# Softmax stage of a four-layer graph network on one core: one product group moved ahead of an exponent product, two groups held back, and one numerator product moved to the end of the sums

## What is computed

```
w_m = (efeat @ W_msg  + b_msg ).reshape(E, 16, 16)
w_a = (efeat @ W_attn + b_attn).reshape(E, 16, 16)
h_src = feat[src][:, :, None]
e1, e2 = w_m * h_src, w_a * h_src
seg_max = segment_max(e2, dst)
ex   = exp(e2 - seg_max[dst])
ft   = segment_sum(e1 * ex / segment_sum(ex, dst)[dst], dst)
out  = ft.sum(axis=1)
```

## Time and profile before

| what | value |
|---|---|
| median of 3 runs | 10814.75 us (10812.35 to 10816.42) |
| the profiled execution | 10814.88 us, span 10812.9 us |
| PE busy | 7709.7 us, 71% |
| DVE busy | 7490.8 us, 69% |
| POOL busy | 8188.1 us, 76% |
| ACT busy | 2807.2 us, 26% |
| mean granted TensorE clock | 0.836 of full |

### The profile page before, as it was taken

How to read it: one execution, slowest core, us unless ns; L and a number is a source line. 1 busy time by engine, 2 the same in 40 slices (tenths; PEclk the granted TensorE clock), 3 DMA queues, 4 the chain that set the end, 5 groups by cost and what they waited for, 6 DMA issues and landing times.

```text
span 10812.9 us, 126451 instructions
## 1 busy us (share of the span) xinstructions
PE 7709.7 (71%) x34167; PEld 3929.5 (36%) x34167; DVE 7490.8 (69%) x13704; ACT 2807.2 (26%) x12100; POOL 8188.1 (76%) x5375
## 2 busy tenths in 40 slices
PE   0999985999946566566666656633999994788884
PEld 0455442555522222222222222211555553344442
DVE  2555551444428999999999999975778883677774
ACT  0111110000016656666666666622000000000000
POOL 5788885777758888888888888853888885788887
PEclk6999986999967777777777777765999996888886
DMA  1333331222216666666666656645222221333332
GB/s 35 97 98 98 91 81 35 62 62 62 62 24 171 172 177 178 173 175 178 174 173 178 175 172 179 176 132 181 72 75 75 75 75 29 100 90 90 90 90 49
DMA packets 501017, 1210.69 MB, mean 112 GB/s; under 512 B 244715, under 2 KB 281743, under 8 KB 480135
## 3 DMA queue, kind: packets, MB, share of 16 engines
q1 hardware_dynamic: 241732, 983.55, 28.5%
q0 software_dynamic: 223712, 118.77, 8.8%
q10 hardware_dynamic: 35440, 106.85, 3.1%
HBM read 415.09 MB, written 787.23 MB: 111 GB/s over the span
## 4 chain that ended last, share of the span: by engine, by line
POOL 37%; PE 27%; ACT 18%; issue 11%; DVE 3%; DMA 2%; SPq 1%; ACTq 0%; DVEq 0%; POOLq 0%
POOL arena L513 37%; ACT arena L726 17%; PE PS L876 10%; PE PS L1010 8%; PE PS L1011 7%; PE PS L898 1%; ACT arena L744 1%; DVE arena L1529 1%; DMA d_rel<-arena 1%; SPq L310 0%; DMA d_nn<-arena 0%; DVE arena L1561 0%; PE PS L987 0%; DVE arena L1525 0%; PE PS L1073 0%
## 5 line engine op out<-in xcount | busy, mean ns | idle before, releaser
L876 PE MATMUL PS<-arena,TB 125*128 125x500 bf16 (+1 forms) x17325 | 4103.1, 384 | 140.8 <-DVE arena L1275 138.9
L513 POOL DMA_INDIRECT arena<-d_feat,srci x1650 | 3204.6, 1942 | 730.4 <-issue 455.1
L513 POOL DMA_INDIRECT arena<-d_h,srci x1584 | 2029.1, 1281 | 697.6 <-issue 472.6
L876 PEld LDWEIGHTS PS<-arena,TB 125*128 125x128 bf16 (+1 forms) x17325 | 1570.0, 100 | 2365.1 <-issue 988.6
L726 ACT ACTIVATE arena<-PS,arena 125x32 f32<-125x32 f32 x10560 | 1934.8, 557 | 44.2 <-DMA arena<-d_feat,srci 44.2
L1010 PE MATMUL PS<-arena,ident 125*125 125x512 f32 x1650 | 1090.4, 749 | 1139.2 <-DVE arena L1529 1137.6
L1286 DVE SCALAR_TENSOR_TENSOR arena<-arena,lane,PS 128x500 f32<-128x500 f16 x825 | 598.0, 725 | 1551.0 <-PE PS L876 1180.8
L513 POOL DMA_INDIRECT arena<-d_rel,irel x858 | 1220.2, 1422 | 429.8 <-issue 261.2
L513 POOL DMA_INDIRECT arena<-d_nn,srci x858 | 1215.4, 1417 | 352.0 <-issue 261.2
L1275 DVE TENSOR_SCALAR arena<-arena,lane 125x1500 bf16<-125x1500 f16 (+1 forms) x1848 | 1191.8, 703 | 183.9 <-PE PS L876 125.5
L1561 DVE SCALAR_TENSOR_TENSOR arena<-arena 125x512 f32<-125x512 f32 x1485 | 1100.1, 741 | 0.4
(11 more groups left out here) (262 smaller groups left out, 5618.1 us busy)
## 6 DMA issues: line engine op xcount, KB each, us to landing
d_soft_den<-arena SPq DMA_DIRECT2D x330, 560.0 KB
d_soft_num<-arena SPq DMA_DIRECT2D x330, 560.0 KB
d_soft_max<-arena SPq DMA_DIRECT2D x165, 1120.0 KB
arena<-d_pick SPq DMA_DIRECT2D x99, 750.0 KB
arena<-d_lane SPq DMA_DIRECT2D x99, 750.0 KB
d_x<-arena ACTq DMA_DIRECT2D x165, 241.7 KB
arena<-d_x SPq DMA_DIRECT2D x165, 241.7 KB
d_rel<-arena SPq DMA_DIRECT2D x50, 669.4 KB
```

Source lines behind the costliest of these rows:

```text
L513: gp.indirect_dma_start(out=dst, out_offset=None, in_=table, in_offset=bass.IndirectOffsetOnAxis(ap=index, axis=0)).then_inc(S(sem), 16)
L876: ins = pe.matmul(PS[0:w, 2048 + (q % 3) * 512:2048 + (q % 3) * 512 + QW], TB[:, part, g * LANES * F:g * LANES * F + w], OH[L][i][:, g, at ...
```

## The change

On PE, the first two product groups of the next block now follow the scalable products of t = 8 and 9 and wait until DVE has done six of the 19 maxima of the current block. The third group moves from ahead of exponent difference n = 5 to ahead of n = 4. On DVE, `weigh(8)` moves from the first place of the sums to behind the sum of t = 7, so two of the interleaved places are empty at the start, and the waits of the sums are lowered by one numerator to match. No instruction is added or removed but waits.

```diff
             def soft(b, s, k, first, left):
                 ahead, k1 = (s + 1) % 3, k + (s == 2)
                 if left >= 1:
+                    for t in range(AT + 2, B1):
+                        scalable(b + 1, ahead, k1, t)
+                    pe.wait_ge(S("soft_max"), MAXES * b + AT)
                     products(b + 1, ahead, k1, 0)
                     products(b + 1, ahead, k1, 1)
-                    for t in range(AT + 2, B1):
-                        scalable(b + 1, ahead, k1, t)
 
                 for n in range(6):
                     if n == 4 and left >= 2:
                         scalable(b + 2, (s + 2) % 3, k + (s >= 1), AT)
-                    if n == 5 and left >= 1:
+                    if n == 4 and left >= 1:
                         products(b + 1, ahead, k1, 2)
...
-                weigh(B1 - 2)
+                yield
                 yield
                 weigh(0)
                 yield
...
-                        dve.wait_ge(S("soft_num"), 5 * b + 2)
+                        dve.wait_ge(S("soft_num"), 5 * b + 1)
...
-                            dve.wait_ge(S("soft_num"), 5 * b + min(t // 2 + 2, 5))
+                            dve.wait_ge(S("soft_num"), 5 * b + t // 2 + 1)
...
-                    if t % 2 and t < B1 - 3:
+                    if t % 2 and t < B1 - 1:
                         weigh(t + 1)
                         yield
```

## The result

The changed kernel takes 10494.74 us (median of 4 runs, 10489.41 to 10501.9) against 10815.58 us, a ratio of 0.9704 with a 95% interval of 0.9687 to 0.9721: 321 us or 3% faster. The forecast was 10815 us, no change. It also lies far outside the range for 8 in 10, 10776 to 10830 us. The time is close to that of the last rival, "VectorE bounds" at 10484 us, which had a chance of 0.02.

A forecast was written before the change was run, and what follows sets the result against it. The prediction took VectorE's and ACT's loops as both tight, with ACT closing the loop. From the profiled 10814.88 us, 0 x 163 + 0.7 - 0.1 gave 10815.5, rounded 10815 us; range for 8 in 10: 10776 to 10830.

The forecast's parts named there:

- VectorE bounds: Rival for the softmax stage: the gain is real, 2.03 us a block go, 331 us, giving 10484 us; chance 0.02.
- What bounds the kernel now: Softmax stage: ACT, 60% busy, closes the block loop of 23.89 us between PE's n = 3 and the maximum of t = 9.
- The 3.0 us of idle forward maxima: VectorE's forward maxima idle only 3.0 us over 2000 us, 84 blocks; read as arriving just as ACT releases them.
- two tight loops: Softmax stage: VectorE's and ACT's loops are both tight, so removing VectorE's wait leaves ACT's loop as it is.
- VectorE's wait, "Gain 0": VectorE's product instructions: the 331.5 us wait goes, but some 2 us a block of idle time appears before the forward maxima.
- The faster: Rival: the clock rises earlier or stays up at PE's differences; period 23.57, mean 23.66 us, gain 37 us, 10778; chance 0.13.
- the slower rival: Rival: PE waits for the first product pair, the exponent of n = 5 is late; period 24.16 us, 10858; chance 0.09.
- Sums before and after: VectorE: two pairs move, so products start 8.75 us after the first backward maximum instead of 7.72.
- Third group: PE, ahead of n = 4: issued 10.17 us after the first backward maximum, new wait 0.18 us, covered by ACT, cost 0.
- Numerators of t = 0: VectorE's `weigh(0)`: the exponent of n = 4 is out by then or 0.1 later, and VectorE has 2 us to give.
- First two groups held back: PE: the groups start after six maxima, where PE is idle; price 0.
- The self-restoring period: Block loop: a shorter block does more differences at 1.2 GHz before the clock's rise and gives the gain back.

The follow-up runs named there:

- the run with 18 repeats: Kernel before with 18 needless repeats of one second-group product on PE, ahead of the second group: 10664.92 us, ratio 0.9847.
- 16 or 18 repeats: Needless repeated products on PE: 16 in the changed kernel between its first two groups, 10466.78 us; 18 in the kernel before, 10664.92 us.

## Why the prediction was wrong

**What bounds the kernel now: the step that failed.** "ACT ... closes the loop, because it must do all of this between PE's n = 3 and the maximum of t = 9." It need not: the scaled values of that stretch are the next block's. The timeline after shows the maximum 2.06 us ahead of ACT's end, and 3.6 us less on ACT changed nothing. What the runs showed in its place is the loop through the third group, with VectorE's wait of 2.03 us on it. The text ahead of the prediction has the right block numbers; the loop was read from the chain of waits and not checked against them. The 3.0 us of idle forward maxima, taken as a sign of two tight loops, were a sign that ACT held nothing up: VectorE waited for nothing there.

**VectorE's wait, "Gain 0".** This is the term that followed from it. The wait was on the loop with its full 2.03 us. The rival that said so priced it at 331 us; 320.7 came. That they lie so close is partly luck. VectorE still waits 34 us between 3300 and 6800 us (18.9 + 8.9 + 5.0 + 1.2), which the rival had at nothing; against that, the 0.28 us of issue gap in a third of the blocks are gone too, and the six products in one run take 3.70 us to the first maximum, where four and then two took 2.48 and 1.32. The 0.02 was the other error: the share of 90% and a wait of the same engine were evidence for it, and the evidence against was one inferred link and the 3.0 us read by its light.

**The faster and the slower rival: both priced by ACT's loop.** Their periods, 23.57 and 24.16 us, add to the exponential of n = 5 the 10.24 us of ACT's stretch that bounds nothing. In the run with 18 repeats the kernel before, with the clock up from n = 0 on, took 22.83 us for a block (M at 4001.95 and at 4024.78).

**Sums before and after: right.** The products start at 4047.75, M at 4039.00: M+8.75, to the digit. Only the 0.28 us gap in every third block, which the forecast carried on, is no longer seen.

**Third group: right in its place.** In that block it was issued at M+10.08, against 10.17 worked out:

```profile
4049.08 0.65 PE L976 MATMUL PS<-arena 99*125 99x512 bf16 x2
```

The exponential of n = 5 came at M+13.45 (4052.45), against 13.39. The new wait behind the first product pair cost next to nothing, and the slower rival did not occur.

**Numerators of t = 0: the cover was smaller than said.** "VectorE has 2 us to give" rested on ACT's loop. VectorE had nothing to give, and the wait, "0.1 later", is up to 0.5 us and the larger part of what the changed kernel still loses (27.8 of the 34 us). The forecast worked it out with some 4.5 us at the low clock in every block; between 4000 and 4400 us the changed kernel has 2.9 to 6.3, and waits in the blocks with the long stretches.

**First two groups held back, at 0: right.** The rule of the Trainium skill, page "TensorE: Matmul & The Clock Gate", section "HAM oscillation — how this bites in real kernels", that closed gaps keep PE at full clock, agrees with these runs only where the gap is really filled: with 16 or 18 repeats the granted clock of the stage was 0.89, with four moved products it stayed at 0.78.

**The self-restoring period: right, but of limited reach.** Added work of 0.43 us vanished in it. A shortening of 1.0 us (the numerators alone) already broke through it, and the low stretch then changed from block to block.

## What to carry to other kernels

A link in the chain of waits is inferred from times. Before a forecast rests on one, look up in the code which block's value it carries, and do it above all where the link makes an engine with 60% load the bound and excuses a 90% one that visibly waits.

A group that waits in one engine's order behind work for another consumer can be worth moving ahead of it; but look at what the freed engine does next. Here the numerators that came right after waited for an exponential, 64.8 us in all, and moving both gave more than the sum of each.

## What the runs showed of the hardware

The granted clock made the time of a loop insensitive to small edits: 0.43 us more PE work in each of 165 blocks left the time where it was (between -0.11% and +0.08%), since the rise then came 0.83 us sooner after the first difference. An edit of that size can measure as nothing in such a kernel and still count once the loop has left that state. Needless matmuls in PE's idle time, 18 a block, made the kernel before 1.5% faster, since the differences then ran at 2.4 GHz in most blocks.
